# The first layer's products with the values in three batches of four units instead of six of two

## What is computed

```python
a1 = _attn(q, k1, v1, causal=True)
a2 = _attn(q, ks, vs, causal=False)
a3 = _attn(q, kw, vw, causal=True)
out = g[:, 0] * a1 + g[:, 1] * a2 + g[:, 2] * a3
return out.transpose(0, 2, 1, 3).reshape(B, T, N_HEAD * V_HEAD) @ w_proj
```

## Time and profile before

| | us |
|---|---|
| median of three runs | 3586.07 (3584.92 to 3587.94) |
| the profiled execution | 3588.78 |
| its span | 3586.9 |
| TensorE (PE) busy | 3273.3 (91%) |
| VectorE (DVE) busy | 1987.1 (55%) |
| ScalarE (ACT) busy | 1567.3 (44%) |
| GpSimd (POOL) busy | 927.5 (26%) |
| mean granted clock of TensorE | 0.941 |

### The profile page before, as it was taken

One profiled execution on the slowest core, in us unless ns is written; L12 is line 12 of the kernel. 1 busy time (PEld: TensorE's weight loads), 2 busy tenths in 40 slices (PEclk: granted clock), 3 DMA queues, 4 the chain that ended last, 5 costly groups with the idle time before them and its releaser, 6 DMA issues.

```text
span 3586.9 us, 58807 instructions
## 1 busy us (share of the span) xinstructions
PE 3273.3 (91%) x20560; PEld 2333.5 (65%) x20560; DVE 1987.1 (55%) x6976; ACT 1567.3 (44%) x3441; POOL 927.5 (26%) x1840
## 2 busy tenths in 40 slices
PE   4999789998899979999899998999889998899978
PEld 3676657765677656776567765677656766567665
DVE  3664565555556465554656546566455554566445
ACT  1444344543454334543445525445253542544424
POOL 0222322222222222222222232222322223222222
PEclk7999899998999989999899998999999998999989
DMA  2000000000000000000000000000000000000000
GB/s 80 30 19 7 6 13 25 19 7 1 19 19 19 7 1 25 19 13 7 1 25 19 13 7 1 31 13 13 6 1 31 19 7 6 13 19 19 7 6 7
DMA packets 31438, 53.75 MB, mean 15 GB/s; under 512 B 3472, under 2 KB 13456, under 8 KB 30864
## 3 DMA queue, kind: packets, MB, share of 16 engines
q1 hardware_dynamic: 31120, 49.64, 4.3%
HBM read 44.91 MB, written 4.72 MB: 14 GB/s over the span
## 4 chain that ended last, share of the span: by engine, by line
PE 79%; DVE 11%; issue 4%; POOL 3%; ACT 2%; PEld 1%; PEldq 1%; SPq 0%; DMA 0%; POOLq 0%; ACTq 0%; DVEq 0%
PE outs L896 14%; PE work L820 7%; PE work L781 7%; PE work L857 6%; PE work L802 6%; PE work L858 5%; PE work L859 5%; PE work L903 4%; PE outs L1007 3%; DVE work L1124 3%; PE work L777 3%; PE work L786 2%; PE work L997 2%; PE work L861 2%; PE work L791 2%
## 5 line engine op out<-in xcount | busy, mean ns | idle before, releaser
L1480 ACT ACTIVATE PR<-work 128x512 f32<-128x512 f32 (+1 forms) x1088 | 640.5, 597 | 580.3 <-PE work L859 477.3
L1124 DVE CUSTOM_DVE_ANT_0 work<-work,KEEPB 128x384 f32<-128x384 f32 (+3 forms) x1536 | 665.5, 480 | 75.5 <-PE work L820 74.1
L1606 POOL TENSOR_SCALAR_AFFINE_SELECT PR<-PR 128x256 f32<-128x256 f32 (+1 forms) x960 | 348.3, 366 | 952.5 <-ACT PR L1480 948.6
L1108 DVE TENSOR_TENSOR BIG<-work,BIG 96x512 fp32r<-96x512 f32 (+1 forms) x455 | 285.4, 629 | 355.0 <-ACT BIG L1375 355.0
L820 PE MATMUL work<-BIG 96*128 96x448 f32 (+9 forms) x1664 | 447.9, 367 | 36.6 <-DVE NMX L1124 15.9
L1596 POOL TENSOR_TENSOR TOK<-AB 128x256 f32<-128x256 f32 (+1 forms) x325 | 219.2, 674 | 877.5 <-DVE AB L1078 854.8
L896 PE MATMUL outs<-PR,ONES 128*32 128x512 f32 (+4 forms) x2304 | 404.5, 458 | 0.0
L857 PE MATMUL work<-BIG 99*128 99x512 f32 (+4 forms) x1152 | 404.5, 351 | 0.0
L820 PEld LDWEIGHTS work<-BIG 96*128 96x128 f32 (+1 forms) x1664 | 285.2, 207 | 174.7 <-issue 91.7
L1077 DVE TENSOR_TENSOR AB<-work,COS 128x256 f32<-128x256 f32 (+2 forms) x357 | 150.0, 420 | 426.9 <-PE work L781 366.3
L858 PE MATMUL work<-BIG 96*128 96x512 f32 (+4 forms) x1152 | 382.4, 332 | 0.0
(11 more groups left out here) (161 smaller groups left out, 5280.9 us busy)
## 6 DMA issues: line engine op xcount, KB each, us to landing
WKW<-w_kw_dram SPq DMA_DIRECT2D x65, 256.0 KB, 2.8
WSEL<-w_sel_dram SPq DMA_DIRECT2D x65, 256.0 KB, 3.0
X<-x_dram SPq DMA_DIRECT2D x9, 512.0 KB, 3.4
out_dram<-X SPq DMA_DIRECT2D x9, 512.0 KB, 2.8
WFC<-w_fc_dram SPq DMA_DIRECT2D x1, 1024.0 KB, 9.9
WFP<-w_ffp_dram SPq DMA_DIRECT2D x1, 1024.0 KB, 11.9
WQKV<-w_qkv_dram SPq DMA_DIRECT2D x1, 768.0 KB, 13.0
WQ<-w_q_dram SPq DMA_DIRECT2D x1, 576.0 KB, 7.4
```

The lines of the kernel that those rows point to most:

```text
L1108: read_work(v.tensor_tensor(dst[1], src, dst[0].bitcast(F32), ALU.subtract), use)
L1124: last = v.tensor_tensor_reduce(ps[:, lo:hi], ps[:, lo:hi], KEEPB[:, T - (hi - lo):T], -1.0, -NEG, ALU.add, ALU.min, dst)
L1480: a.activation(PR[0:rows, j % NP, :], ps[0:rows, :], ACT.Exp).then_inc(exp_ready, 1)
L1606: gp.affine_select(blocks, blocks, [[0, len(cols)], [1, P]], ALU.is_ge, 0.0, base=0, channel_multiplier=-1).then_inc(exp_masked, 1)
```

## The change

In `units0` the units that hold A1's key tile 2 and A3's key tile 2 move from places 8 and 9 to places 4 and 5, so that all of A1 is in units 0 to 5. `PV[0]` becomes three batches of four units: units 0 to 3 (A1 tiles 0, 1, 3), 4 to 7 (A1 tile 2, A3 tiles 0 and 2), 8 to 11 (A3 tiles 1 and 3, A2). A1 is complete after the second batch, A3 and A2 after the third; their steps `out` and `out_tr` are set 0.1 and 0.4 units apart (`late`). TensorE waits before a batch for the last mask in it and, if the last unit has none, for its exponential too. The waits for the copied output banks, the `stop` flags (`LAST`) and ScalarE's waits for the batches follow. The same products are computed.

In TensorE's order, the steps of pair 5 after the last batch of pair 4 become: piece_tr 3, unit 2, piece_tr 4, unit 3, piece_tr 5, piece_tr 6, out_tr A3, unit 4, out_tr A2, max 0, unit 5, max 1, max 2, batch 0, max 3, unit 6, max 4, 5, 6, unit 7, max 7, 8, 9, unit 8, max 10, 11, unit 9, piece 0, batch 1, unit 10, and A1's out_tr after unit 11. At the end of pair 7: unit 9, batch 1, unit 10, unit 11, out_tr A1, batch 2, out_tr A3, out_tr A2, projection.

```diff
@@ -86,8 +86,8 @@
-    for what in ([(A1, 0, 0)], [(A1, 1, 0), (A1, 3, 384)], [(A3, 0, 0)], [(A3, 1, 0), (A3, 3, 384)],
-                 [(A1, 2, 0), (A3, 2, 256)], [(A2, 0, 0)]):
+    for what in ([(A1, 0, 0)], [(A1, 1, 0), (A1, 3, 384)], [(A1, 2, 0), (A3, 2, 256)],
+                 [(A3, 0, 0)], [(A3, 1, 0), (A3, 3, 384)], [(A2, 0, 0)]):
@@ -114,12 +114,13 @@
-PV = [[(2 * k, 2 * k + 1) for k in range(6)], [(0, 1), (2, 3), (4,)]]
+PV = [[tuple(range(4 * k, 4 * k + 4)) for k in range(3)], [(0, 1), (2, 3), (4,)]]
...
-COMPLETE = [{4: [A1, A3], 5: [A2]}, {2: [0]}]
+LAST = [{A1: 2, A3: 3, A2: 0}, {0: 2}]
+COMPLETE = [{1: [A1], 2: [A3, A2]}, {2: [0]}]
@@ -168,15 +169,15 @@
-            for a in COMPLETE[layer].get(k, []):
+            for late, a in enumerate(COMPLETE[layer].get(k, [])):
...
-                t1 = t + 0.3 + o["tr"]
-                at += [(t + 0.3, ("out", what, a)), (t1, ("out_tr", what, a)), (t1 + 0.1, ("norm", what, a))]
+                t1 = t + 0.3 + 0.4 * late + o["tr"]
+                at += [(t + 0.3 + 0.1 * late, ("out", what, a)), (t1, ("out_tr", what, a)), (t1 + 0.1, ("norm", what, a))]
@@ -866,13 +867,13 @@
-                if units[-1] in CAUSAL[layer]:
-                    pe.wait_ge(exp_masked, MASK0[layer] + p * len(CAUSAL[layer]) + CAUSAL[layer].index(units[-1]) + 1)
-                else:
+                masked = [CAUSAL[layer].index(i) for i in units if i in CAUSAL[layer]]
+                pe.wait_ge(exp_masked, MASK0[layer] + p * len(CAUSAL[layer]) + masked[-1] + 1)
+                if units[-1] not in CAUSAL[layer]:
                     pe.wait_ge(exp_ready, UNIT0[layer] + p * NU[layer] + units[-1] + 1)
-                if layer == 0 and p and k in (0, 2, 5):
-
-                    pe.wait_ge(evacuated, 3 * (p - 1) + {0: A1, 2: A3, 5: A2}[k] + 1)
+                if layer == 0 and p:
+
+                    pe.wait_ge(evacuated, 3 * (p - 1) + [A1, A3, A2][k] + 1)
@@ -894,7 +895,7 @@
-                                      start=(j == 0), stop=(j == 2 or a == A2), skip_group_check=True)
+                                      start=(j == 0), stop=(j == LAST[layer][a]), skip_group_check=True)
@@ -1457,7 +1458,7 @@
-                    act.wait_ge(pv_done, PV0[0] + n * NPV[0] + (6 if att == A2 else 5))
+                    act.wait_ge(pv_done, PV0[0] + n * NPV[0] + (2 if att == A1 else 3))
```

## The result

The changed kernel takes 3613.8 us (median of four runs, 3612.1 to 3624.7) against 3586.1 for the kernel before in the same comparison: ratio 1.0085, 95% interval 1.007 to 1.01. The profiled execution has 3614.5 us and a span of 3612.6. It is slower, as forecast, but by 28 us and not by 16.

A forecast was written before the change was run, and what follows sets the result against it. TensorE's own queue was taken to bound the first-layer attention stretches. Edges saved 29 us and waits added 45, +16 net: 3602 us median, 8-in-10 range 3567 to 3616; the forecast's own case, 3594 to 3614, had 50%.

The forecast's parts named there:

- The three waits I listed: Bank and copy waits at unit 4, unit 8 and the end of pair 7; 5.6 us per sequence, +45 us.
- Rivals B and C: Bank waits at units 4 and 8: B, don't form, 3566 to 3578, 25%; C, half of each wait, 3584, 17%.
- rival D: Batches keep their edges so only waits are left, 3631, or one wait at the maxima doubles, 3620; together 8%.
- The edges: Entering and leaving batches of value products, six made three per pair; saves 3.65 us per sequence, 29 us in all.
- First place: Score unit 4 waits for a work bank read by ScalarE then VectorE; 0.45 us in pairs 1 to 6.
- the other waits are met: Across the changed order, waits for value slots, output banks and masks were taken to cost nothing.
- Second place: Unit 8 waits 0.40 for VectorE's maximum 6, maximum 9 0.05; 0.45 in pairs 0, 1, 3, 5, 1.8 per sequence.
- Third place: End of pair 7: 0.3 us wait for exponential 11, 0.77 for output copies; 1.1 per sequence.
- TensorE's idle time: First-layer attention stretches: idle time goes from 0.05 us to some 5 us each, part possibly hidden.

## Why the prediction was right or wrong

**Right: the direction and its cause.** The change takes cover away from places where banks are late and puts it where they aren't. The three waits I listed are where I put them, and each goes when what makes it is moved. Rivals B and C (waits that don't form, or half of them) fall with the table of pairs; the first half of rival D (the edges stay) falls with the batch cut apart. Its second half, a doubled wait at the maxima, is nearer: that wait is 0.57 to 0.78 in the pairs where I had 0.45. In the head pairs I had 5.6 - 3.65 = 1.95 a sequence, 16 us; they are 30 longer. Of the 15 us missing, 13 are a wait that I didn't list, and a wait that I sized too small adds 10; the other terms take 8 back.

**The edges**. I had 3.65 a sequence. The pairs are 3.79 longer with some 7.7 of new waits (below), so the edges gave back about 3.9. This is a remainder and not a measurement of its own: if the wait ahead of maximum 0 is read from the distances (0.92 in pair 0, 0.54 in pair 6) and not from what the move took away, it is 4.4. Pair 5 alone went from 31.28 to 31.80 with 1.06 of waits, so the edges gave 0.54 there, where I had 0.45. The sum is right to that, but partly by luck: an edge is 0.34 and not 0.2 where a maximum product follows, as behind batch 2, so the removed edges elsewhere gave less. Batch 0 stood ahead of the 64-row transposes, which now pay their own change of array shape: transposes 5 and 6 keep their starts, 0.54 and 0.24 apart, with the batch gone from between. The Trainium skill (TensorEngine Tiling (Array Packing), Key Properties: a change of the tiling mode drains the engine) is borne out in both places where I weighed it: the joint within the third batch costs 0.13 (1.995 us against 1.860 for four units of one shape), and the transposes keep about 0.1.

**First place**. Forecast: unit 4 at 4.08 after transposes 3, wanted at 3.6, wait 0.45. Measured: at 4.06 (716.44 to 720.50), wanted at 3.76, wait 0.30, and 0.33 won by the move of the copy. The chain over ScalarE and VectorE was forecast to 0.02; what was off is TensorE's own side: transposes 5 and 6 and the output transposes take 0.79 + 0.41 = 1.20, where I had 0.45 + 0.61 = 1.06. An error of 0.16 in a sum of 3.7 is a third of the wait, since a wait is a difference of two long sums. It is 1.9 a sequence (between the 1.8 of the distances and the 2.0 that the move won) and not 2.7.

**Missed: maximum 0.** The step of my forecast that failed is "the other waits are met". It lists value slots, output banks and masks, and not the wait of maximum 0 for the readers of the next pair's transposed pieces, of which VectorE's low part of transposes 6 is the last. Batch 0 and the output transposes stood ahead of maximum 0 and covered it, just as they covered unit 4. In the kernel before, pair 0 already waited for it 0.24 us: unit 4 to maximum 0 takes 1.02 there (559.07 to 560.09) and 0.78 in other pairs (716.49 to 717.27 in pair 5). That was to be seen:

```profile
559.07 0.50 PE L857 MATMUL work<-BIG 99*128 99x512 f32 x1
...
560.09 0.45 PE L820 MATMUL work<-BIG 96*128 96x448 f32 x1
```

With the change it is 0.2 in pairs 1 to 5, 0.26 in pair 6 and 0.72 in pair 0, by what the move took away: 1.9 a sequence, 1.65 of it new, or 13 us. The other misses (first place -0.8 a sequence, second +1.2, edges -0.25) nearly cancel, and the rest of the launch, 4.6 us shorter in the profiled execution, hides a few us of the miss: so the forecast of the time is 12 us short. That 16 was not further from 28 is partly luck.

**Second place**. Unit 8 was forecast at 2.65 after maximum 4 and came at 2.60 (726.34 to 728.94). (The prediction's 1.56 is maxima 4 to 6 and unit 7; maxima 7 and 8 are its 0.58. Its sum is right.) The wait at unit 8 is 0.34, near the forecast 0.40. But maximum 9 waits 0.13, not 0.05, and maximum 10 another 0.10, as VectorE is behind for the banks that follow too: 0.57 a pair in pairs 1, 3, 5, where I had 0.45. In pair 0 it is 0.78, as unit 8 is followed only after 1.08 there (0.92 in the others) and maximum 10 after 0.31 (0.26). And pairs 2, 4 and 6 aren't quite free (0.18 each, of 0 forecast). This term was sized too small: 3.0 a sequence and not 1.8.

**Third place**. Forecast 0.3 + 0.77, measured 0.36 + 0.79. Right.

In sum the waits are 1.9 + 1.9 + 3.0 + 1.15, some 8 a sequence, 0.25 of which the kernel before had; forecast 5.6. The Trainium skill (TensorEngine Tiling (Array Packing), PSUM Bottleneck: tiling speeds TensorE up and leaves the evacuation of PSUM as it is) points the same way, though no run here changes the tiling itself: at unit 4, at unit 8 and at the last output transposes TensorE stands for a bank or a copy that ScalarE or VectorE gives back too late, while these two are busy for only half of the time (118.5 and 130.9 of 243.3 us).

**What would have shown it.** I wrote that TensorE's idle time would be some 5 us a stretch, part of it hidden. 3.3 us are printed, 2.6 more than before, of some 8: most are hidden behind modelled ends. The distances between starts carry the whole of it. In the prediction's own stretch, which ends before the end of pair 7, the idle time is only 1.6 us (549.30 to 778.20).

**Open.** In pair 6 VectorE begins the low part of transposes 5 some 0.35 us later after its high part than in the other pairs, though idle. I didn't find for what it waits; the move of maximum 0 hides half of it. That the rest of the launch was 4.6 us shorter in the profiled execution of after lies within what it varies by (last section); nothing was tried on it.

## What to carry to other kernels

Work that is taken out of the bounding engine's queue was also cover for the banks and data that other engines were making. Before merging or moving such work, list for each instruction right behind the place every wait that stands ahead of it (for data as well as for buffers), and who ends it last; then move those producers, or move the consumer one step back, and ask whether it needs all that it waits for. Here the merge alone lost 28 us, and the merge with four steps moved by at most two places was 16 us faster than the kernel before (3572.2 against 3588.1).

## What the runs showed of the hardware

In this kernel one more batch of products on 32-column tiles, between maximum products, cost 0.34 us beyond its columns (0.09 entering, 0.14 leaving, 0.10 behind), 0.2 of which can be read off the starts of one batch alone. Two batches side by side cost no more than one, signal included: 1.00 + 0.99 us against 1.99 with 128-row and then 64-row products, and pair 7 within 0.02 us of the changed kernel with the first batch in halves of the same row count. The rest of the launch outside these stretches, which no experiment edited, took between 1663 us (at a mean clock of 0.947) and 1676 us (at 0.940) in the profiled executions. The unedited kernel alone varies as much: sixteen runs of it lay between 3580.2 us (mean clock 0.946) and 3594.3 us (0.939). That is why differences under some 5 us were read from the head pairs and not from the total.
